# A fused gated cross-attention and mixture-of-experts block: the last token group's routing in two halves, and one of three expert sums closed and loaded earlier

## What is computed

```python
logits = x @ w_router
probs = softmax(logits);  w_topk, sel = top_k(probs, 4)       # 32 experts, 4 per token
pos = rank of the token within its expert, in order of tokens  # kept if pos < CAP = 128
buf[e, pos] = x[tok]                                           # 128 slots per expert
y = (silu(buf @ w_gate) * (buf @ w_up)) @ w_down               # per expert, F = 176
out[tok] += w * y[e, pos]                                      # sum over a token's experts
sh = sigmoid(x @ w_shared_gate) * ((silu(x @ sw_gate) * (x @ sw_up)) @ sw_down)   # FS = 704
return inp + out + sh
```

## Time and profile before

| | us |
|---|---|
| median of 3 runs (lowest 311.15, highest 312.66) | 311.17 |
| profiled execution, its own time | 310.34 |
| its span in the trace | 308.6 |
| TensorE busy in the span | 270.6 (88%) |
| VectorE busy | 203.4 (66%) |
| GpSimd busy | 192.0 (62%) |
| ScalarE busy | 122.5 (40%) |

### The profile page before, as it was taken

How to read it: one execution, slowest core, us unless ns; L and a number is a source line. 1 busy time by engine, 2 the same in 40 slices (tenths; PEclk the granted TensorE clock), 3 DMA queues, 4 the chain that set the end, 5 groups by cost and what they waited for, 6 DMA issues and landing times.

```text
span 308.6 us, 4993 instructions
## 1 busy us (share of the span) xinstructions
PE 270.6 (88%) x1482; PEld 220.8 (72%) x1482; DVE 203.4 (66%) x586; ACT 122.5 (40%) x342; POOL 192.0 (62%) x265
## 2 busy tenths in 40 slices
PE   1977658989989989899699898899999999999980
PEld 0876548968877878797578676677777777778750
DVE  2589999896689989679927321245554554456685
ACT  2358346764759000666046600443333333321100
POOL 2899975938989785882777676036666666662200
PEclk9999997999999999999799999999999999999997
DMA  6899996999721020110299700539999999578899
GB/s 209 230 301 341 298 249 224 343 344 309 250 81 43 38 86 30 65 52 34 74 255 271 208 17 0 155 81 247 257 258 254 267 296 281 79 137 220 185 353 312
DMA packets 53322, 59.65 MB, mean 193 GB/s; under 512 B 6744, under 2 KB 48920, under 8 KB 53296
## 3 DMA queue, kind: packets, MB, share of 16 engines
q1 hardware_dynamic: 42336, 47.24, 51.0%
q0 software_dynamic: 7680, 8.95, 14.7%
q10 hardware_dynamic: 3280, 3.15, 3.0%
HBM read 36.83 MB, written 27.21 MB: 208 GB/s over the span
## 4 chain that ended last, share of the span: by engine, by line
PE 43%; DVE 26%; DMA 10%; issue 7%; ACT 7%; POOL 3%; SPq 1%; DVEq 0%; ACTq 0%; POOLq 0%
PE Y L1230 12%; DVE arena L798 7%; PE pg L1075 5%; PE pd L1249 4%; DMA expert_sum<-arena,ide 4%; PE Y L1249 4%; PE pu L1075 3%; DVE x_sb L999 3%; PE Y L1221 2%; DMA arena<-in_ctx_dram 2%; DVE arena L783 2%; PE pm L1240 2%; DVE arena L788 2%; DVE arena L790 2%; PE pg L1108 2%
## 5 line engine op out<-in xcount | busy, mean ns | idle before, releaser
L396 POOL DMA_INDIRECT dispatched<-rows,dsu x64 | 63.4, 990 | 26.4 <-issue 18.7
L473 POOL DMA_INDIRECT expert_sum<-arena,ide x32 | 49.6, 1550 | 46.6 <-DVE arena L989 38.0
L798 DVE TENSOR_REDUCE arena<-arena 128x128 f32<-128x1024 f32 x32 | 38.7, 1211 | 0.2
L1063 PE MATMUL Y<-arena 128*128 128x144 f32 x128 | 27.7, 299 | 12.6 <-DVE arena L790 11.0
L976 DVE TENSOR_TENSOR arena<-arena,Y 128x176 f32<-128x176 f32 x32 | 10.8, 337 | 37.6 <-ACT arena L698 37.6
L1063 PEld LDWEIGHTS Y<-arena 128*128 128x128 f32 x128 | 20.3, 192 | 17.1 <-issue 11.9
L691 ACT ACTIVATE arena<-Y,wn 128x128 f32<-128x128 f32 x64 | 20.0, 364 | 29.6 <-PE Y L1221 29.5
L552 ACT ACTIVATE silu<-pg 128x512 f32<-128x512 f32 x20 | 11.9, 595 | 48.7 <-PE pg L1075 48.7
L808 DVE TENSOR_TENSOR act<-silu,pu 128x512 f32<-128x512 f32 x20 | 13.7, 686 | 24.5 <-PE pu L1075 16.5
L1065 PE MATMUL Y<-arena 128*128 128x144 f32 x128 | 26.4, 289 | 0.0
L1064 PE MATMUL Y<-arena 128*128 128x144 f32 x128 | 26.2, 287 | 0.0
(11 more groups left out here) (180 smaller groups left out, 647.0 us busy)
## 6 DMA issues: line engine op xcount, KB each, us to landing
expert_sum<-zrow SPq DMA_DIRECT2D x3, 2176.0 KB, 14.8
dispatched<-zrow SPq DMA_DIRECT2D x1, 4624.0 KB, 22.2
arena<-dispatched SPq DMA_DIRECT2D x32, 144.5 KB, 3.7
arena<-expert_sum SPq DMA_DIRECT2D x16, 256.0 KB, 5.6
arena<-in_L_ffn_w_gate_dram SPq DMA_DIRECT2D x18, 176.0 KB, 4.1
arena<-in_L_ffn_w_up_dram SPq DMA_DIRECT2D x18, 176.0 KB, 4.7
arena<-in_L_ffn_w_down_dram SPq DMA_DIRECT2D x18, 176.0 KB
first_slots<-in_L_ffn_w_gate_dram SPq DMA_DIRECT2D x14, 176.0 KB, 4.2
```

Source lines behind the costliest of these rows:

```text
L396: pool.indirect_dma_start(buf, bass.IndirectOffsetOnAxis(ap=dsu[:, t % 2, j:j + 1], axis=0), rows[:, t % 2, j // K, :], None, bounds_check ...
L473: pool.indirect_dma_start(accs[a], bass.IndirectOffsetOnAxis(ap=ide[:, e % NO:e % NO + 1], axis=0), ye[:, e % NO, :], None, compute_op=ALU ...
L798: dve.tensor_reduce(oT[:, g % 2, :, 2 * HD * p:2 * HD * (p + 1)].rearrange("l e (a j) -> l a e j", a=2), Z[:, p % 2].rearrange("l (a e) j ...
L1063: pe.matmul(yv[:, 0], TT[:, h, P:L], kvv[:, 0], start=True, stop=True)
```

## The change

Four things are changed, and nothing else of the program.

1. The chain of the last group is split in two halves of two batches (`last_stats(h)`, `last_pow(h)`, `last_shift(h)`, `last_rows(h)`, `last_transposes(h)`, `last_evac(h)`, `last_logits(h)`, `last_lg(h)`, `last_top(h)`, `last_rank(h)`, `last_slots(h)`, `last_gates(h)`, `last_exp(h)`), the second half's ranks counting the first's, and interleaved with units 18 to 22.
2. The third group's chain (t = 2) lies one to two steps earlier within the eight steps of group 3; the second half of its turned rows gets the bank `pd`.
3. POOL's sends are written in another order: the last seven pairs of group 1 between the products, then five pairs of group 2, the two powers of the last group, the other three pairs, and the last group's eight pairs with a wait for each half.
4. `CLOSE` is 24: sum 2 is closed by expert 23, and experts 24 to 31 alternate between sums 0 and 1. Sum 2 is loaded in eight parts of 256 KB, part i issued when expert 24 + i has been scaled (at the latest 31). From expert 27 (`MIX`) on DVE adds one part of it after each expert, five in all, and the other three between the last units.

```diff
-CLOSE = 27
+CLOSE, LOAD2, MIX = 24, 25, 27
...
         def late_bank(t, half):
-            if half and t in (0, G - 1):
+            if half and t != 1:
                 return pd if t else pu
             return pm
...
-        FINE = (2, 2, 1)
+        FINE = (2, 2, 2)
...
-            load_sum(2)
-            load_sum(0)
-            load_sum(1)
+            for i in range(2 * G):
+                sp.wait_ge(s["e_yout"], min(LOAD2 + i, E))
+                load_sum(2, i)
+            for a in range(2):
+                for i in range(2 * G):
+                    load_sum(a, i)
...
+            def last_pow(h):
+                pool.wait_ge(s["x1_ready"], G + h)
+                b2 = slice(2 * h, 2 * h + 2)
+                pool.tensor_tensor(rs[:, :, b2], vs[:, :, b2], neg_half[:].rearrange("p (a b) -> p a b", a=2)[:, :, b2], ALU.pow
+                                   ).then_inc(s["powed"], 1)
...
             t = G - 1
-            token_rows(t)
-            xn_evac(t, 0)
-            xn_evac(t, 1)
+            last_rows(0)
+            last_evac(0)
+            last_rows(1)
+            last_lg(0)
             silu(LATE + 2)
-            lg_copy(t)
+            last_exp(0)
+            last_evac(1)
+            last_lg(1)
+            last_gate()
+            last_exp(1)
+            silu(LATE + 3)
             for c in range(2):
-                xn_high(t, c)
-            silu(LATE + 3)
-            last_exps(t)
+                last_high(c)
             silu(LATE + 4)
...
             use(LATE - 1)
+            use(LATE)
             x1(t, 0)
+            last_stats(0)
             x1(t, 1)
-            token_stats(t)
-            token_vars(t)
-            use(LATE)
-            token_shift(t)
+            last_shift(0)
+            last_stats(1)
             use(LATE + 1)
-            top(t)
-            shift(t)
-            top_masks(t)
+            last_shift(1)
+            last_top(0)
+            last_slots(0)
+            last_gates(0)
             use(LATE + 2)
-            token_slots(t)
+            last_top(1)
+            last_slots(1)
+            last_gates(1)
+            last_shared_gate()
             use(LATE + 3)
-            token_gates(t)
             last_low(t)
...
                 e_yout(e)
-            dve.wait_ge(s["base_ready"], G)
-            dve.wait_ge(s["down_used"], GB * (G - 1))
-            for k in range(G):
-                pair_mark[0, 2 * k] = mark(add_sum(2, 2 * k))
-                use(UNITS_END[k])
-                pair_mark[0, 2 * k + 1] = mark(add_sum(2, 2 * k + 1))
+                if e == MIX:
+                    dve.wait_ge(s["base_ready"], G)
+                    dve.wait_ge(s["down_used"], GB * (G - 1))
+                if e >= MIX:
+                    pair_mark[0, e - MIX] = mark(add_sum(2, e - MIX))
+            for i in range(E - MIX, 2 * G):
+                use(UNITS_END[i - (E - MIX)])
+                pair_mark[0, i] = mark(add_sum(2, i))
+            use(UNITS_END[2 * G - (E - MIX)])
...
+            unit(LATE)
             out_tr(t, 0)
             out_tr(t, 1)
-            unit(LATE)
             unit(LATE + 1)
-            xn_transposes(t, 0)
-            xn_transposes(t, 1)
+            last_transposes(0)
+            last_logits(0)
             gate(2, 0)
-            logits(t)
+            last_transposes(1)
+            last_rank(0)
             up(2, 0)
             gate(2, 1)
-            rank(t)
+            last_logits(1)
             up(2, 1)
+            last_rank(1)
```

More of the change, by code:

```diff
@@ L435, in _ @@
                 ins.then_inc(s["w_low"], 1)
-            for g in range(1, G):
+            for g in range(1, G - 1):
                 t = g - 1
@@ L595, in exps, with last_rows @@
                 act_e.activation(ez[:], ez[:], ACT.Copy, bias=1.0).then_inc(s["exp_done"], 1)
-            def last_exps(t):
-                act_e.wait_ge(s["lg_ready"], t + 1)
+            def last_rows(h):
+                t = G - 1
+                act_e.wait_ge(s["nb_ready"], G + h)
+                act_e.wait_ge(disp_sem[t - 2], 16 * GB * K)
+                for b in range(2 * h, 2 * h + 2):
+                    act_e.activation(rows[:, t % 2, b, 0:L], x_sb[:, GB * t + b], ACT.Identity,
+                                     bias=nb1[:, b:b + 1], scale=rs[:, 1, b:b + 1])
+                at = GB * t + 2 * h
+                act_e.activation(rows[:, t % 2, 2 * h:2 * h + 2, L + E], tok[:, at:at + 2], ACT.Copy).then_inc(s["xn_ready"], 1)
@@ L632, in _ @@
             query(2, 0)
-            for g in range(1, G):
+            for g in range(1, G - 1):
                 t = g - 1
                 for p in range(NP_):
-                    if p < 4 and g + 1 < G:
+                    if p < 4:
                         k_evac(g + 1, p)
@@ L1197, in _ @@
                         xn_transposes(t, 1)
+            g, t = G - 1, G - 2
+            for p in range(NP_):
+                if p < NP_ - 1:
+                    conv(g, p + 1)
+                if p == 0:
+                    out_tr(t, 0)
+                    out_tr(t, 1)
+                if p == 3:
+                    logits(t)
+                if p == 4:
+                    rank(t)
+                unit(UNIT_AT[g, p])
+                if p == 2:
+                    xn_transposes(t, 0)
+                    xn_transposes(t, 1)
@@ new lines, in last_transposes, with last_logits @@
+            def last_transposes(h):
+                t = G - 1
+                pe.wait_ge(s["xn_ready"], G + h)
+                for c in range(2):
+                    for i in range(2):
+                        ins = pe.transpose(late_bank(t, h)[:, (2 * c + i) * S:(2 * c + i + 1) * S],
+                                           rows[:, t % 2, 2 * h + i, c:L:2], ident[:])
+                ins.then_inc(s["xn_tr"], 1)
+            def last_logits(h):
+                t = G - 1
+                pe.wait_ge(s["xnT_f"], 2 * t + 2 * h + 2)
+                for i in range(2):
+                    b = 2 * h + i
+                    for c in range(2):
+                        ins = pe.matmul(late_bank(t, h)[:, i * NR:(i + 1) * NR], xnT_f[:, c, b * S:(b + 1) * S], wr[:, c, :],
+                                        start=(c == 0), stop=(c == 1))
+                ins.then_inc(s["lg_done"], 1)
@@ L1198, in _, with last_rank @@
+            def last_rank(h):
+                pe.wait_ge(s["m_ready"], G + h)
+                for i in range(2):
+                    b = 2 * h + i
+                    o = late_bank(G - 1, h)[:, i * E:(i + 1) * E]
+                    ins = pe.matmul(o, tri[:], M[:, b, :], start=True, stop=(b == 0))
+                    for a in range(b):
+                        ins = pe.matmul(o, ones[:], M[:, a, :], start=False, stop=(a == b - 1))
+                ins.then_inc(s["rank_done"], 1)
             t = G - 1
+            unit(LATE)
```

178 lines of the change are left out of this document (151 added, 27 removed).

## The result

The changed kernel took 313.54 us in the median of 20 runs, the kernel before 311.47 in 20 runs beside them: a ratio of 1.0069, 95% interval 1.0048 to 1.0090. It is slower, by 0.7%; I had forecast 308.8. Its profiled execution took 313.38 (span 311.6), 3.0 more than that of before. A ratio leaves out runs that lie more than 1.5% above the shortest of their kernel, which matters for e5 and e9.

A forecast was written before the change was run, and what follows sets the result against it. DVE's convolution bounds up to about 150, TensorE through the experts, transfers at the end. Gains of 0.4 (front) and 1.95 (tail), 2.35 together, gave 308.8 against the median of 311.17; range 306.9 to 312.2.

The forecast's parts named there:

- Third group sooner, sends reordered: Third group's chain and POOL's sends: last send some 6 us sooner, units 16 and 17 still ending about 147.7.
- gains nothing: Claim that sooner third-group sends bring no time, TensorE being the bound; they remain only as cover if TensorE gets faster.
- The last group's chain in halves: Front, from about 147.7 to the first expert: splitting the chain starts the first expert at 196.6, a gain of 0.4.
- my walk: Step-by-step timing of the last group's split chain from 147.7: out_tr at 150.6, half rows ready at 156.0, TensorE resuming 156.05.
- the sum of waits, 5.9: TensorE's waits from 154.3 to the first expert: 1.75 + 1.0 + 0.5 + 1.15 + 0.75 + 0.78.
- The rival on the clock: TensorE's clock falls in the new waits of 1.75 and 1.0: 1.3 lost, 310.1; chance 0.25.
- A gain of 0.4: Front term: first expert at 196.6 instead of 197.01 through the last group's chain in halves.
- My estimate by that figure: ACT's two table loads on the path, priced at the page's 2.66 us per switch: 0.4 gain becomes 1.9 loss.
- Sum 2 earlier and paced: Tail: with sum 2 closed sooner and loaded in parts, expert 30's add lands at 286.0, 1.95 before 287.95.
- my lower bound: Landing of an add in the tail beside nothing: 3.79, bound by the experts' pace, a gain of 3.4.
- The crowded case: Rival in the tail: adds crowd in two sums, landings take 6.1, tail +2.1, time 312.9; chance 0.12.
- Sends: POOL's 64 sends: last one out some 6 us sooner, gaining nothing; rival that they were the bound, 302.8, chance 0.02.

The follow-up runs named there:

- e5: Kernel before with six extra subtractions on POOL that nothing reads, ahead of group 2's sends, where DVE does that group's slots; ratio 1.0056 to the kernel before.
- e9: Changed kernel with the last group's chain whole again, as in the kernel before, on all four engines; ratio 1.0048 to the kernel before.
- e1: Changed kernel with POOL's two subtractions for the third group moved ahead of sends, away from DVE's comparison; ratio 0.9952 to the kernel before.
- e10: e7 with the last group's chain whole again, as in the kernel before, on all four engines; ratio 0.9889 to the kernel before.
- e3: Kernel before with only the third sum's part of the change (sum 2 closed earlier, loaded in parts, added in the expert loop); ratio 0.9936.
- e7: Changed kernel with DVE's third-group slots one step later and three instead of five pairs of sends ahead of the last powers; ratio 0.9910 to before.
- e6: Changed kernel with 34 unread turnings of the identity keeping TensorE busy ahead of the last convolution piece; ratio 1.0032 to the kernel before.
- e11: e8 with DVE's use(22), use(23), ACT's silu(23), and use(19) with unit 20's gate moved ahead of chain steps; ratio 0.9809 to the kernel before.
- e8: e7 with TensorE's units ahead of the last group's chain links, ACT's and DVE's lists following; ratio 0.9879 to the kernel before.

## Why the prediction was wrong

**The step that failed** is "Third group sooner, sends reordered": that units 16 and 17 end where they did, about 147.7, "since TensorE has the same work ahead of them and DVE's steps only change places". Unit 18, behind them, began at 151.41. A step that changes places also changes what runs beside it. The comparison, 0.29 where it stood, cost 3.18 at its new place, beside POOL's two subtractions; its stretched row at 103.25 lay on the chain that ended last before, and I priced DVE's steps as if each cost the same anywhere. With that collision taken out (e1) `out_tr` is at 150.23, where I had it at 150.6. Whether this part, without the collision, "gains nothing" stays open: e10 against e3 points to 0.5 at the first expert, within what can be told apart.

**The last group's chain in halves.** Unit 18 filled the wait of 2.56 as forecast, and the half rows came 5.5 behind `out_tr`, as in my walk (156.05 less 150.6; its terms there add up to 155.9). Of the sum of waits, 5.9, the changed kernel has 1.64, 0.93, 0.26, 1.05, 0.51 and 0.78: 5.2. The rival on the clock happened beside the forecast: half clock for about 3.4 us behind the waits of 1.64 and 0.93, a loss of some 1.7 where that rival had 1.3. So 46.0 from `out_tr` to the first expert became 47.3. A gain of 0.4 stood on the forecast; e10 against e7 gives none, e9 against the changed kernel a loss of 2.0. On the two loads of a function table the row held; the drain of 1.38 of which the Trainium skill (ScalarE: Activation LUTs, What ACT_TABLE_LOAD costs) tells does not show. My estimate by that figure was wrong too: two drains of 1.38 make 2.8, a loss of 2.4 and not 1.9. Load and next function, timeline of ACT, 160 to 176, as in the earlier trace rows:

```profile
165.91 1.28 ACT L666 ACT_TABLE_LOAD   x1
167.21 0.26 ACT L666 ACTIVATE ex<-ex 128x64 f32<-128x64 f32 x1
```

The start of the next function is again 1.30 behind that of the load. The Trainium skill (TensorE: Matmul & The Clock Gate, Why this matters for your kernels) advises against long idle gaps between bursts of matmuls. The trace agrees behind the wait of 4.55, where e6 measured the price, 1.5; the waits of 1.64 and 0.93 are each shorter than the gaps it warns of.

**Sum 2 earlier and paced.** Right in mechanism and nearly in size. I assumed landings of 4.5 for the adds of experts 24, 26 and 28; the chain has 5.00, 3.98 and 4.78, mean 4.59. Expert 30's add starts 16.2 behind expert 24's, forecast 15.75. In e3 the adds keep the experts' pace, nearer to my lower bound, and the part brings 2.0 by the ratio. The crowded case did not come.

**Sends.** POOL's last send went out at 188.35, 2.1 sooner than in the earlier trace rows and not some 6, since POOL stood idle for 4.92 ahead of the last group's first power (157.40). No gain came of it, as forecast: TensorE was the bound. They became the bound in e11, once TensorE's waits were gone.

## What to carry to other kernels

When a step is moved, look up what every other engine does at the place it goes to, and search the trace for instances of the same instruction that took longer than the rest: the one that did names the neighbour that it must not have. A wait of TensorE can cost twice, once by its length and once by the clock behind it, so when TensorE is the bound its units stand ahead of the links of any chain that has slack, and the slack is read at the next bound (here the sends, 13 us ahead of the first expert).

## What the runs showed of the hardware

An operation of DVE with both inputs in SBUF waited for POOL's arithmetic through several operations in a row: two (2.54 us) in the changed kernel, what was left of six in e5, ending 0.16 us behind the last of them in both. At 103.25 in the kernel before it ended at 105.01, 0.15 behind the last but one of eight. A copy from SBUF to SBUF was held in the same way, 1.50 in e1 and 1.74 before, instead of 0.17. Operations of the same engine with an input in PSUM went on beside POOL's arithmetic (e5), and POOL's sends held no comparison: that of the last group's first half in the changed kernel, of 64 columns, took 0.22 at 166.49, within the send at 166.31. The Trainium skill (SBUF — State Buffer, SBUF: two separate sides) states that GpSimd and an operation of DVE with two SBUF inputs, or in a mode that uses two ports, exclude each other on a shared pair of ports, for a whole instruction; the traces agree for the operations with two SBUF inputs, but here the loser waited for more than one instruction. That the copy ran in such a mode no run here shows.

TensorE's clock was at 0.50 not only behind the wait of 4.55 (in e9 0.6 us after work began again) but also behind pairs of short waits with little work between them: 1.64 and 0.93 in the changed kernel and in e1, 1.14 and 0.81 in e11. In e8, with unit 20's gate between the 1.64 and the next link, it stayed at 1.00. Behind a single wait of about 2 it is not settled: it fell behind 2.56 before and 2.20 in e8, stayed at 1.00 behind 2.10 in e1, and behind the same wait of 1.83 for the whole rows it fell in e10 and stayed in e9.
